# An LSTM over 512 steps: two of four gates computed with the weights stationary

## The chip, the cores and the metric

The kernel runs on one core of a Trainium2 chip. The metric is device time of one execution in microseconds, lower is better. All times below are in us unless marked ns. PE is TensorE, DVE is VectorE, ACT is ScalarE, SP is SyncE; PEld is PE's load of a stationary operand.

## The reference

`x` has shape (4, 512, 256), four sequences of 512 steps of 256 features; `h0` is `cond_1024`, (4, 256). All is f32.

```python
xW = jnp.einsum('ntd,dk->tnk', x, Wx) + b          # Wx: (256, 1024)
def step(carry, xw_t):
    prev_h, prev_c = carry
    a = xw_t + prev_h @ Wh                          # Wh: (256, 1024)
    i, f, o = sigmoid(a[:, 0:256]), sigmoid(a[:, 256:512]), sigmoid(a[:, 512:768])
    g = tanh(a[:, 768:1024])
    next_c = f * prev_c + i * g
    next_h = o * tanh(next_c)
    return (next_h, next_c), next_h
out = x + hs
```

Each step needs the one before it; the input product `x @ Wx` does not.

## The kernel before, in words

**Layout.** A 256 wide vector is cut into four quadrants of 64 units (Q = 4), each of two halves of 32 (M = 2). "By rows" a tile has partition 32q + 4t + n for quadrant q, step t of a chunk and sequence n, and 64 columns, the units of the quadrant. "By units" partition 32q + r holds unit r of quadrant q and the columns are steps and sequences. DVE's 32x32 block transpose (L296) turns the first into the second. Eight steps of four sequences fill 32 partitions, so a chunk is eight steps (STEPS), and there are 64 chunks.

**The input product.** For a whole chunk at once PE computes `x_acc` (L346) from `x_units` and `wx`, in four pieces (PIECES) behind steps 3 to 6 of the chunk before. DVE adds the bias at step 7 (`make_x_part`, L235). At the end of step 7 PE injects the result into the four PSUM banks `gates[k]` with an identity as stationary operand (`inject`, L355), once a bank's last turn is done. SP loads `x_next` and `x_here` and stores `y_rows`, each as four DMAs a chunk (L149, L154, L160).

**A step on PE** (L360 to L383). The banks are F, A, B, O; A holds G and I of half 0, B holds G and I of half 1. `recur(b, k)` takes half b of h as stationary operand (a window of `h_pad` of 32 columns in which the four of this step stand at the right place and the others are zero) and streams 64 columns of `wh`, one matmul for each of four 32-column tiles of the array.
**A step on DVE** (L280 to L327). Its order is written out: turn F, turn A, turn B (L296), `forget` (L301, it forms (tanh_f + 1) times half of c), turn O, `update(0)`, `update(1)` (a scan that gives the new cell state, L307), `hidden(0)`, `hidden(1)` (the new h into `h_pad`, L314). Step 0 begins with `turn_back` of the chunk before (L270), step 1 with `residual` (L277), step 2 with the turn of the next x (L290), step 7 with `make_x_part`. `update` waits for ACT's tanh of I and G (L305) and for `forget` (L306).

**A step on ACT** (L199 to L216). tanh_f for both halves (L203), tanh of G and I of half 0 and of half 1 (L210), tanh_o (L212), tanh of the cell for each half (L215), and half of c kept for the next step (L216). Sigmoids are tanh with halved weights. Eight instructions a step, in this order, each behind its semaphore.

Of the kernel before, what the change touches and what calls it, by code (L numbers as in the profile page):

```python
# [5 lines left out]
def lstm_residual_kernel(nc: bass.Bass, x: bass.AP, cond: bass.AP, w_x: bass.AP, w_h: bass.AP, bias: bass.AP,  # L6
                         out: bass.AP):

# [18 lines left out]
    BF, BA, BB, BO = range(4)  # L27
    BANKS = (BF, BA, BB, BO)
    GC = len(BANKS) * W
# [5 lines left out]

    PIECES = [(b, slice(c * GC // 2, (c + 1) * GC // 2)) for b in range(M) for c in range(2)]
    FIRST_PIECE_AT = 3

    ctx = ExitStack()
    with ctx:  # L40
# [12 lines left out]
        wh = sb("wh", [128, M, Q, GC])  # L53
        bias_raw = sb("bias_raw", [128, NG, QD])
# [8 lines left out]
        x_part = sb("x_part", [128, GC])  # L63

# [12 lines left out]
        gates = [ps(f"gates{k}", [128, 512]) for k in BANKS]  # L77
        x_acc = ps("x_acc", [128, 512])
        turned_bank = [ps(f"turned_bank{k}", [128, 512]) for k in range(3)]
        turned = [turned_bank[k][:, 0:W] for k in (0, 1, 2)] + [turned_bank[0][:, W:2 * W]]  # L80
        tanh_c = [turned_bank[AB[m]][:, W:W + N] for m in range(M)]
# [17 lines left out]
        x_part_made = sem("x_part_made")  # L99
        h_turned_back = sem("h_turned_back")  # L100
        y_made = sem("y_made")
        y_stored = sem("y_stored")

        gates_done = [sem(f"gates_done{k}") for k in BANKS]
        gates_turned = [sem(f"gates_turned{k}") for k in BANKS]
        tanh_f_done = sem("tanh_f_done")
        tanh_ig_done = [sem(f"tanh_ig_done{m}") for m in range(M)]
        kept_done = sem("kept_done")
        forgotten = sem("forgotten")
# [74 lines left out]
        def _(act):  # L184
# [34 lines left out]
        def _(dve):  # L219
# [8 lines left out]

            def permute_matrix(made, raw, b, factor, loaded):
# [24 lines left out]
            permute_matrix(wh, wh_raw, 0, 0.5, wh_loaded).then_inc(wh_made, 1)  # L254
            dve.wait_ge(bias_made, 1)
            make_x_part(0)
            permute_matrix(wh, wh_raw, 1, 0.5, wh_loaded).then_inc(wh_made, 1)

# [21 lines left out]
            def step(chunk, t, first, ahead):  # L280
# [10 lines left out]
                if ahead and t == STEPS - 1:  # L291
                    make_x_part(chunk + 1)

# [4 lines left out]
                def forget():  # L298

                    dve.wait_ge(tanh_f_done, now)  # L300
                    nc.vector.scalar_tensor_tensor(out=scan_both[:, :, K * N + K - 1:2 * K * N:K], in0=tanh_f[:], scalar=1.0,  # L301
                                                   in1=half_d[:], op0=ALU.add, op1=ALU.mult).then_inc(forgotten, 1)
# [36 lines left out]
        def _(pe):  # L339
# [45 lines left out]
            for piece in PIECES:  # L385
                x_product(*piece, 0)
# [33 lines left out]
```

## Time and profile before

| | |
|---|---|
| median of 3 runs | 1100.56 us (1094.28, 1100.56, 1101.48) |
| the profiled execution | 1090.95 us |
| its span, first to last instruction | 1089.2 us |
| granted TensorE clock, mean | 0.963 |
| busy: PE, PEld, DVE, ACT | 697.3, 574.9, 790.8, 550.4 us |

The time of a run is taken around the program, the span within it. The engines overlap, so busy times don't add up to the span. PE's clock is granted at one of two levels, 2.4 GHz (1.0) or 1.2 GHz (0.5).

### The profile page before, as it was taken

The page shows a single profiled execution, that of the slowest core. Times are in us where ns is not written, and L with a number is a line of the kernel's source. Part 1 is how long each engine was busy: PE and PEld are TensorE (multiplying, and loading weights), DVE is VectorE, ACT ScalarE, POOL GpSimd, SP SyncE. Part 2 cuts the span into 40 slices and gives each one's busy share as a digit, 9 for nine tenths or more (in the row PEclk, how much of TensorE's full clock was granted, in tenths as well). Part 3 has the DMA queues.
Part 4 walks back from the last instruction along what each step waited for, and adds up shares of the span by engine and source line. Part 5 has one row for each costly group of instructions (what it writes and reads, how often), then busy time and mean ns, then how long its engine had stood idle before and what let it go on. Part 6 is the DMA issues. An engine that isn't in the chain of part 4 may idle for free.

```text
span 1089.2 us, 88137 instructions
## 1 busy us (share of the span) xinstructions
PE 697.3 (64%) x36864; PEld 574.9 (53%) x36864; DVE 790.8 (73%) x4897; ACT 550.4 (51%) x3586; POOL 0.7 (0%) x6
## 2 busy tenths in 40 slices
PE   4666666666666666666666666667666666766664
PEld 3555555555555555555555555555555555545554
DVE  4777777777777777777776777776777777777776
ACT  2455555555545555555554555554545555455554
POOL 0000000000000000000000000000000000000000
PEclk9999999999999999999998999998999998999999
DMA  3000000000000000000000000000000000000000
GB/s 89 5 7 5 6 6 6 6 6 5 7 5 6 7 5 5 6 6 6 6 6 6 5 6 7 5 6 6 6 6 6 6 6 6 5 6 6 6 6 7
DMA packets 32110, 8.74 MB, mean 8 GB/s; under 512 B 31584, under 2 KB 31584, under 8 KB 32096
## 3 DMA queue, kind: packets, MB, share of 16 engines
q1 hardware_dynamic: 31488, 8.41, 3.5%
q10 hardware_dynamic: 608, 0.14, 0.1%
q8 instruction: 9, 0.15, 0.1%
q14 instruction: 5, 0.04, 0.0%
HBM read 6.43 MB, written 2.10 MB: 8 GB/s over the span
## 4 chain that ended last, share of the span: by engine, by line
DVE 51%; PE 24%; ACT 14%; issue 8%; SPq 1%; DVEq 1%; DMA 0%
DVE turned_bank L296 39%; PE gates L364 24%; DVE h_pad L314 8%; ACT tanh_o L212 8%; ACT turned_bank L215 7%; DVE scan_both L301 3%; DVE cell L307 1%; DVEq L330 1%; SPq L139 1%; DVE h_rows L270 0%; DMA wh_raw<-in_L_cond_Wh_dram 0%; SPq L143 0%; DVEq L269 0%; DVE wh L225 0%; DVE wh L222 0%
## 5 line engine op out<-in xcount | busy, mean ns | idle before, releaser
L364 PE MATMUL gates<-wh,h_pad 128*32 128x64 f32 x32768 | 591.2, 227 | 374.8 <-DVE h_pad L314 373.3
L364 PEld LDWEIGHTS gates<-wh,h_pad 128*32 128x32 f32 x32768 | 506.5, 114 | 488.3 <-DVE h_pad L314 486.4
L296 DVE STREAM_TRANSPOSE turned_bank<-gates 128x64 f32<-128x64 f32 x2048 | 478.5, 262 | 182.3 <-PE gates L364 170.0
L203 ACT ACTIVATE tanh_f<-turned_bank 128x8 f32<-128x8 f32 x512 | 90.7, 177 | 438.1 <-DVE turned_bank L296 427.6
L210 ACT ACTIVATE scan_both<-turned_bank 128x8 f32<-128x8 f32 x1024 | 185.1, 181 | 59.9 <-DVE turned_bank L296 17.3
L314 DVE SCALAR_TENSOR_TENSOR h_pad<-tanh_o,turned_bank 128x4 f32<-128x4 f32 x1024 | 132.7, 158 | 74.2 <-ACT turned_bank L215 4.6
L307 DVE TENSOR_TENSOR_SCAN cell<-scan_both 128x12 f32<-128x12 f32 x1024 | 144.0, 181 | 2.1 <-issue 0.3
L215 ACT ACTIVATE turned_bank<-cell 128x4 f32<-128x4 f32 x1024 | 143.3, 172 | 2.5 <-DVE cell L307 0.3
L346 PE MATMUL x_acc<-wx,x_units 128*32 128x128 f32 x2048 | 107.5, 285 | 9.3 <-DVE x_units L249 9.3
L212 ACT ACTIVATE tanh_o<-turned_bank 128x8 f32<-128x8 f32 x512 | 90.7, 177 | 28.9 <-DVE turned_bank L296 6.7
L216 ACT ACTIVATE half_d<-cell 128x8 f32<-128x8 f32 x512 | 100.4, 196 | 0.0
L301 DVE SCALAR_TENSOR_TENSOR scan_both<-tanh_f,half_d 128x8 f32<-128x8 f32 x512 | 77.8, 152 | 0.0
L355 PE MATMUL gates<-x_part,ident 128*32 128x64 f32 x2048 | 57.1, 230 | 1.8 <-DVE x_part L235 1.8
L346 PEld LDWEIGHTS x_acc<-wx,x_units 128*32 128x32 f32 x2048 | 50.4, 115 | 9.3 <-DVE wx L227 9.3
L355 PEld LDWEIGHTS gates<-x_part,ident 128*32 128x32 f32 x2048 | 40.6, 109 | 10.6 <-issue 2.2
L270 DVE STREAM_TRANSPOSE h_rows<-h_pad 128x64 f32<-128x64 f32 x64 | 15.7, 246 | 26.0 <-DVE h_pad L314 25.6
L235 DVE TENSOR_TENSOR x_part<-x_acc,bias_rows 128x256 f32<-128x256 f32 x64 | 26.7, 418 | 0.0
L290 DVE STREAM_TRANSPOSE x_units<-x_next 128x64 f32<-128x64 f32 x63 | 15.5, 246 | 0.0
L277 DVE SCALAR_TENSOR_TENSOR y_rows<-h_rows,x_here 128x64 f32<-128x64 f32 x64 | 14.4, 225 | 0.0
L222 DVE TENSOR_SCALAR wx<-wx_raw 128x256 f32<-128x256 f32 x2 | 0.6, 294 | 5.2 <-DMA wx_raw<-in_L_cond_Wx_dram 5.2
L193 ACT ACT_TABLE_LOAD x1 | 1.3, 1283 | 4.2 <-issue 4.2
L222 DVE TENSOR_SCALAR wh<-wh_raw 128x256 f32<-128x256 f32 x2 | 0.6, 294 | 3.0 <-DMA wh_raw<-in_L_cond_Wh_dram 3.0
(24 smaller groups left out, 6.7 us busy)
## 6 DMA issues: line engine op xcount, KB each, us to landing
x_next<-in_x_dram SPq DMA_DIRECT2D x256, 8.0 KB
x_here<-in_x_dram SPq DMA_DIRECT2D x256, 8.0 KB
out_dram<-y_rows SPq DMA_DIRECT2D x256, 8.0 KB
wx_raw<-in_L_cond_Wx_dram SPq DMA_DIRECT2D x8, 128.0 KB, 3.4
wh_raw<-in_L_cond_Wh_dram SPq DMA_DIRECT2D x8, 128.0 KB, 2.7
bias_raw<-in_L_cond_b_dram ACTq DMA_DIRECT2D x4, 32.0 KB, 3.1
h_rows<-in_cond_dram ACTq DMA_DIRECT2D x4, 1.0 KB
```

Of the source, the lines that this page charges most:

```text
L203: nc.scalar.activation(tanh_f[:], of_step(BF, t), ACT.Tanh).then_inc(tanh_f_done, 1)
L210: nc.scalar.activation(ig, of_step(AB[m], t), ACT.Tanh).then_inc(tanh_ig_done[m], 1)
L212: nc.scalar.activation(tanh_o[:], of_step(BO, t), ACT.Tanh)
L215: nc.scalar.activation(tanh_c[m], cell[:, m, :, K - 1], ACT.Tanh, scale=0.5).then_inc(tanh_done[m], 1)
L216: nc.scalar.activation(half_d[:], cell[:, :, :, K - 1], ACT.Copy, scale=0.5).then_inc(kept_done, 1)
L296: nc.vector.transpose(turned[k], gates[k][:, 0:W]).then_inc(gates_turned[k], 1)
L301: nc.vector.scalar_tensor_tensor(out=scan_both[:, :, K * N + K - 1:2 * K * N:K], in0=tanh_f[:], scalar=1.0, in1=half_d[:], op0=ALU.add, op ...
L307: nc.vector.tensor_tensor_scan(cell[:, m, :, :].rearrange("p n k -> p (n k)"), scan_in[m][:, 0:K * N], scan_in[m][:, K * N:2 * K * N], 0.0 ...
L314: nc.vector.scalar_tensor_tensor(out=h_at(m, t), in0=tanh_o[:, m, :], scalar=1.0, in1=tanh_c[m], op0=ALU.add, op1=ALU.mult).then_inc(h_don ...
L346: last = nc.tensor.matmul(x_acc[q * R:(q + 1) * R, columns], x_units[:, b * R:(b + 1) * R], wx[:, b, q, columns], start=opens, stop=b == M ...
L355: nc.tensor.matmul(gates[k][q * R:(q + 1) * R, 0:W], ident[:, q * R:(q + 1) * R], x_part[:, columns_of(k)], start=True, stop=False, tile_p ...
L364: last = nc.tensor.matmul(gates[k][q * R:(q + 1) * R, 0:W], h_stationary(b, t), wh[:, b, q, columns_of(k)], start=False, stop=b == M - 1, ...
```

## The change

F and O are computed by units: blocks of `wh` of 32 columns are the stationary operand and the four columns of h of this step are streamed. The result stands in PSUM by units in four banks of its own, one per gate and half, and needs no turn. F keeps four tiles of 32 columns; O takes two tiles of 64 columns, from a second copy of its weights, `wh_o`. A and B (I and G) stay by rows. A is turned to PSUM, B to SBUF, and so is the tanh of the cell of half 1. The x part of F and O is turned once a chunk (`turn_x_part`). F's tanh and `forget` are split by half. PE's order in a step is new, the x product has two calls instead of four pieces (behind steps 3 and 4), and `make_x_part` moves from step 7 to step 6. The two waits ahead of the scan change places. Of the pairs of load and matmul that a step has (64 before), 32 are left by rows, 32 are F by units and 16 are O by units.

Names, PSUM and buffers:

```diff
-    BF, BA, BB, BO = range(4)
+    BA, BB, BF, BO = range(4)
+    ROWS = (BA, BB)
-    PIECES = [(b, slice(c * GC // 2, (c + 1) * GC // 2)) for b in range(M) for c in range(2)]
-    FIRST_PIECE_AT = 3
+    X_PRODUCT_AT = (3, 4)
+    X_PART_AT = STEPS - 2
+    UNIT_COLUMNS = slice(GC - 4 * R, GC)
...
-        gates = [ps(f"gates{k}", [128, 512]) for k in BANKS]
+        gates = {k: ps(f"gates{k}", [128, 512]) for k in ROWS}
+        f_units = [ps(f"f_units{m}", [128, 512]) for m in range(M)]
+        o_units = [ps(f"o_units{m}", [128, 512]) for m in range(M)]
...
+        turned = {BA: a_bank[:, 0:W], BB: sb("turned_b", [128, W])[:]}
+        tanh_c = [a_bank[:, W:W + N], sb("tanh_c1", [128, N])[:]]
```

A step on ACT:

```diff
-                    act.wait_ge(gates_turned[BF], now)
-                    nc.scalar.activation(tanh_f[:], of_step(BF, t), ACT.Tanh).then_inc(tanh_f_done, 1)
                     for m in range(M):
+                        act.wait_ge(f_done[m], now)
+                        nc.scalar.activation(tanh_f[:, m, :], f_units[m][:, t * N:(t + 1) * N], ACT.Tanh).then_inc(tanh_f_done[m], 1)
                         act.wait_ge(gates_turned[AB[m]], now)
...
-                    act.wait_ge(gates_turned[BO], now)
-                    nc.scalar.activation(tanh_o[:], of_step(BO, t), ACT.Tanh)
                     for m in range(M):
+                        act.wait_ge(o_done[m], now)
+                        nc.scalar.activation(tanh_o[:, m, :], o_units[m][:, t * N:(t + 1) * N], ACT.Tanh).then_inc(o_tanh_done, 1)
                         act.wait_ge(cell_done[m], now)
```

On DVE:

```diff
+            def turn_x_part(chunk):
+                dve.wait_ge(x_part_made, chunk + 1)
+                nc.vector.transpose(x_part_units[:], x_part[:, UNIT_COLUMNS]).then_inc(x_part_turned, 1)
...
-                if ahead and t == STEPS - 1:
+                if ahead and t == X_PART_AT:
                     make_x_part(chunk + 1)
+                if ahead and t == X_PART_AT + 1:
+                    turn_x_part(chunk + 1)
...
                 def update(m):
+                    dve.wait_ge(forgotten[m], now)
                     dve.wait_ge(tanh_ig_done[m], now)
-                    dve.wait_ge(forgotten, now)
...
-                turn(BF)
                 turn(BA)
+                forget(0)
                 turn(BB)
-                forget()
-                turn(BO)
                 update(0)
+                forget(1)
                 update(1)
                 hidden(0)
                 hidden(1)
```

A step on PE:

```diff
+                def units(b, bank, k, m):
+                    at = k * W + m * R
+                    for q in range(Q):
+                        last = nc.tensor.matmul(bank[q * R:(q + 1) * R, t * N:(t + 1) * N], wh[:, b, q, at:at + R],
+                                                h_at(b, t - 1), start=False, stop=b == M - 1,
+                                                tile_position=(0, q * R), skip_group_check=True)
+                    return last
+
+                def o_part(b, m):
+
+                    for p in range(Q // 2):
+                        last = nc.tensor.matmul(o_units[m][p * 2 * R:(p + 1) * 2 * R, t * N:(t + 1) * N],
+                                                wh_o[:, b, m, p * 2 * R:(p + 1) * 2 * R],
+                                                h_at(b, t - 1), start=False, stop=b == M - 1,
+                                                tile_position=(0, p * 2 * R), skip_group_check=True)
+                    return last
+
                 pe.wait_ge(h_done[0], now)
-                recur(0, BF)
+                rows(0, BA)
+                units(0, f_units[0], BF, 0)
+                rows(0, BB)
                 pe.wait_ge(h_done[1], now)
-                recur(1, BF).then_inc(gates_done[BF], 1)
-                for k in (BA, BB, BO):
-                    recur(0, k)
-                    recur(1, k).then_inc(gates_done[k], 1)
-                if t == STEPS - 1 and ahead:
-                    pe.wait_ge(x_part_made, chunk + 2)
-                    for k in BANKS:
+                rows(1, BA).then_inc(gates_done[BA], 1)
+                units(1, f_units[0], BF, 0).then_inc(f_done[0], 1)
+                rows(1, BB).then_inc(gates_done[BB], 1)
+                units(0, f_units[1], BF, 1)
+                units(1, f_units[1], BF, 1).then_inc(f_done[1], 1)
+                if t == 0:
+                    for m in range(M):
+                        inject_o(m)
+                for m in range(M):
+                    o_part(0, m)
+                    o_part(1, m).then_inc(o_done[m], 1)
+                if ahead and t in X_PRODUCT_AT:
+                    x_product(X_PRODUCT_AT.index(t), chunk + 1)
+                if ahead and t == STEPS - 1:
+                    for k in ROWS:
                         pe.wait_ge(gates_turned[k], now)
-                        inject(k)
-                if ahead and 0 <= t - FIRST_PIECE_AT < len(PIECES):
-                    x_product(*PIECES[t - FIRST_PIECE_AT], chunk + 1)
+                    for m in range(M):
+                        pe.wait_ge(tanh_f_done[m], now)
+                    pe.wait_ge(x_part_turned, chunk + 2)
+                    inject_early()
```

`rows(b, k)` is `recur(b, k)` under a new name. `inject_early` injects A and B by rows (16 pairs) and F by units (16 pairs); `inject_o` injects one half of O with two 64-column tiles (4 pairs). Both use the identity. Ahead of the first step DVE also makes `wh_o` (two instructions) and turns the first x part.

## Rows read from the trace of the kernel before

**Rows 1.** The page: the span, and each engine's busy time and instructions

```profile
span 1089.2 us, 88137 instructions
PE 697.3 (64%) x36864; PEld 574.9 (53%) x36864; DVE 790.8 (73%) x4897; ACT 550.4 (51%) x3586; POOL 0.7 (0%) x6
```

**Rows 2.** The page: chain that ended last, shares of the span by line

```profile
DVE turned_bank L296 39%; PE gates L364 24%; DVE h_pad L314 8%; ACT tanh_o L212 8%; ACT turned_bank L215 7%; DVE scan_both L301 3%; DVE cell L307 1%; DVEq L330 1%; SPq L139 1%; DVE h_rows L270 0%; DMA wh_raw<-in_L_cond_Wh_dram 0%; SPq L143 0%; DVEq L269 0%; DVE wh L225 0%; DVE wh L222 0%
```

**Rows 3.** Order of time, one step: start, duration, engine, line, operation [idle before]

```profile
502.12 0.26 DVE L314 SCALAR_TENSOR_TENSOR h_pad<-tanh_o,turned_bank 128x4 f32<-128x4 f32 x2
...
502.33 0.94 PEld L364 LDWEIGHTS gates<-wh,h_pad 128*32 128x32 f32 x64 [1.08 <-DVE h_pad L314]
502.33 1.10 PE L364 MATMUL gates<-wh,h_pad 128*32 128x64 f32 x64 [0.92 <-DVE h_pad L314]
502.83 0.71 DVE L296 STREAM_TRANSPOSE turned_bank<-gates 128x64 f32<-128x64 f32 x3 [0.26 <-PE gates L364]
503.13 0.18 ACT L203 ACTIVATE tanh_f<-turned_bank 128x8 f32<-128x8 f32 x1 [0.81 <-DVE turned_bank L296]
503.36 0.40 ACT L210 ACTIVATE scan_both<-turned_bank 128x8 f32<-128x8 f32 x2
503.45 0.15 DVE L301 SCALAR_TENSOR_TENSOR scan_both<-tanh_f,half_d 128x8 f32<-128x8 f32 x1
503.50 0.27 DVE L296 STREAM_TRANSPOSE turned_bank<-gates 128x64 f32<-128x64 f32 x1
503.71 0.28 DVE L307 TENSOR_TENSOR_SCAN cell<-scan_both 128x12 f32<-128x12 f32 x2
503.80 0.18 ACT L212 ACTIVATE tanh_o<-turned_bank 128x8 f32<-128x8 f32 x1
503.93 0.28 ACT L215 ACTIVATE turned_bank<-cell 128x4 f32<-128x4 f32 x2
504.14 0.26 DVE L314 SCALAR_TENSOR_TENSOR h_pad<-tanh_o,turned_bank 128x4 f32<-128x4 f32 x2
```

**Rows 4.** Order of time, cut at 502.385: loads begun by then

```profile
502.33 0.16 PEld L364 LDWEIGHTS gates<-wh,h_pad 128*32 128x32 f32 x8 [1.08 <-DVE h_pad L314]
```

**Rows 5.** Order of time, step 3: a piece of the x product

```profile
505.27 0.40 PE L346 MATMUL x_acc<-wx,x_units 128*32 128x128 f32 x8
```

**Rows 6.** Order of time, eight steps apart and around a chunk's end

```profile
498.09 0.26 DVE L314 SCALAR_TENSOR_TENSOR h_pad<-tanh_o,turned_bank 128x4 f32<-128x4 f32 x2
...
512.54 0.42 DVE L235 TENSOR_TENSOR x_part<-x_acc,bias_rows 128x256 f32<-128x256 f32 x1
...
513.46 0.77 PEld L355 LDWEIGHTS gates<-x_part,ident 128*32 128x32 f32 x32
...
514.38 0.26 DVE L314 SCALAR_TENSOR_TENSOR h_pad<-tanh_o,turned_bank 128x4 f32<-128x4 f32 x2
...
515.23 0.58 DVE L296 STREAM_TRANSPOSE turned_bank<-gates 128x64 f32<-128x64 f32 x3
```

**Rows 7.** Three stretches (engines' busy time, granted clock); two turns in the second

```profile
core 0: us, PE busy (x) PEld busy (x) DVE busy (x) ACT busy (x) POOL busy (x), PEclk, DMA share, GB/s
517.41:520.82 3.41, 1.58 (x100) 1.25 (x92) 2.73 (x18) 2.15 (x14) 0.00 (x0) 1.00 0.03 7
520.83:524.24 3.41, 3.00 (x108) 2.54 (x104) 1.70 (x10) 1.01 (x7) 0.00 (x0) 0.50 0.03 7
513.99:517.40 3.41, 2.29 (x136) 1.90 (x134) 2.42 (x18) 1.57 (x12) 0.00 (x0) 1.00 0.00 0
...
521.25 0.27 DVE L296 STREAM_TRANSPOSE turned_bank<-gates 128x64 f32<-128x64 f32 x1 [0.56 <-PE gates L364]
...
521.67 0.27 DVE L296 STREAM_TRANSPOSE turned_bank<-gates 128x64 f32<-128x64 f32 x1 [0.16 <-PE gates L364]
```

**Rows 8.** Order of time: the first and the last step's hidden state

```profile
17.73 0.25 DVE L314 SCALAR_TENSOR_TENSOR h_pad<-tanh_o,turned_bank 128x4 f32<-128x4 f32 x2 [0.18 <-ACT turned_bank L215]
...
1083.94 0.26 DVE L314 SCALAR_TENSOR_TENSOR h_pad<-tanh_o,turned_bank 128x4 f32<-128x4 f32 x2
```

More of the change, by code:

```diff
@@ L63, in lstm_residual_kernel @@
         x_part = sb("x_part", [128, GC])
+        x_part_units = sb("x_part_units", [128, UNIT_COLUMNS.stop - UNIT_COLUMNS.start])
         tanh_f = sb("tanh_f", [128, M, N])
@@ L99, in lstm_residual_kernel @@
         x_part_made = sem("x_part_made")
+        x_part_turned = sem("x_part_turned")
         h_turned_back = sem("h_turned_back")
@@ L254, in _ @@
             permute_matrix(wh, wh_raw, 0, 0.5, wh_loaded).then_inc(wh_made, 1)
+            make_wh_o(0).then_inc(wh_made, 1)
             dve.wait_ge(bias_made, 1)
             make_x_part(0)
+            turn_x_part(0)
             permute_matrix(wh, wh_raw, 1, 0.5, wh_loaded).then_inc(wh_made, 1)
+            make_wh_o(1).then_inc(wh_made, 1)
             dve.wait_ge(h0_loaded, Q * DMA)
@@ L296, in turn, with forget @@
                     nc.vector.transpose(turned[k], gates[k][:, 0:W]).then_inc(gates_turned[k], 1)
[L298 to L302, printed above, removed]
+                def forget(m):
+                    dve.wait_ge(tanh_f_done[m], now)
+                    nc.vector.scalar_tensor_tensor(out=scan_in[m][:, K * N + K - 1:2 * K * N:K], in0=tanh_f[:, m, :], scalar=1.0,
+                                                   in1=half_d[:, m, :], op0=ALU.add, op1=ALU.mult).then_inc(forgotten[m], 1)
                 def update(m):
+                    dve.wait_ge(forgotten[m], now)
                     dve.wait_ge(tanh_ig_done[m], now)
-                    dve.wait_ge(forgotten, now)
                     nc.vector.tensor_tensor_scan(cell[:, m, :, :].rearrange("p n k -> p (n k)"), scan_in[m][:, 0:K * N],
@@ L339, in _, with x_product @@
         def _(pe):
-            def x_product(b, columns, chunk):
-                opens = (b, columns) == PIECES[0]
-                if opens:
+            def x_product(b, chunk):
+                if b == 0:
                     pe.wait_ge(x_turned, chunk + 1)
                 for q in range(Q):
-                    last = nc.tensor.matmul(x_acc[q * R:(q + 1) * R, columns], x_units[:, b * R:(b + 1) * R],
-                                            wx[:, b, q, columns], start=opens, stop=b == M - 1,
+                    last = nc.tensor.matmul(x_acc[q * R:(q + 1) * R, 0:GC], x_units[:, b * R:(b + 1) * R],
+                                            wx[:, b, q, :], start=b == 0, stop=b == M - 1,
                                             tile_position=(0, q * R), skip_group_check=True)
-                if (b, columns) == PIECES[-1]:
+                if b == M - 1:
                     last.then_inc(x_acc_done, 1)
@@ L357, in inject, with inject_units, inject_o @@
                                      tile_position=(0, q * R), skip_group_check=True)
+            def inject_units(bank, k, m):
+                at = k * W + m * R - UNIT_COLUMNS.start
+                for q in range(Q):
+                    nc.tensor.matmul(bank[q * R:(q + 1) * R, 0:R], ident[:, q * R:(q + 1) * R],
+                                     x_part_units[:, at:at + R], start=True, stop=False,
+                                     tile_position=(0, q * R), skip_group_check=True)
+            def inject_o(m):
+                at = BO * W + m * R - UNIT_COLUMNS.start
+                for p in range(Q // 2):
+                    nc.tensor.matmul(o_units[m][p * 2 * R:(p + 1) * 2 * R, 0:R], ident[:, p * 2 * R:(p + 1) * 2 * R],
+                                     x_part_units[:, at:at + R], start=True, stop=False,
+                                     tile_position=(0, p * 2 * R), skip_group_check=True)
@@ L359, in step, with inject_early, rows @@
+            def inject_early():
+                for k in ROWS:
+                    inject(k)
+                for m in range(M):
+                    inject_units(f_units[m], BF, m)
             def step(chunk, t, ahead):
                 now = chunk * STEPS + (t + 1)
-                def recur(b, k):
+                def rows(b, k, columns=slice(0, W)):
                     for q in range(Q):
-                        last = nc.tensor.matmul(gates[k][q * R:(q + 1) * R, 0:W], h_stationary(b, t),
-                                                wh[:, b, q, columns_of(k)], start=False, stop=b == M - 1,
+                        last = nc.tensor.matmul(gates[k][q * R:(q + 1) * R, columns], h_stationary(b, t),
+                                                wh[:, b, q, k * W + columns.start:k * W + columns.stop],
+                                                start=False, stop=b == M - 1,
```

40 lines of the change are left out of this document (25 added, 15 removed).

## The prediction

> **What bounds the kernel now.** I read the page first, then the chain, then the order of time of one step. The page shows no full engine: DVE is busy 73% of the span, PE 64%, ACT 51% [rows 1]. So it is a chain of latencies, and the chain that ended last names it: DVE's turns (L296) 39%, PE's gate matmuls 24%, then short pieces of ACT and DVE [rows 2]. The page can mislead here: DVE's turns carry the name, but the order of time shows what paces them. In one step (PE's first load at 502.33 is my zero) the three turns that follow one another take 0.71 for durations of 0.27, so they start 0.22 apart [rows 3]. At a chunk's start, where PE is ahead, three turns take 0.58, which is 0.155 apart [rows 6]. DVE could do it in 0.155; it waits for PE. PE runs 64 load-and-matmul pairs in 1.10: a round of four column tiles every (1.10 - 0.24)/15 = 0.057, I use 0.056; a gate is four rounds, 0.22 [rows 3]. The fourth turn (503.50) is also where PE's sixteenth round lets it start: 0.03 + 16 x 0.056 + 0.25 = 1.18 after zero. The 0.25 is the time from the end of a round to the turn, from the first one: 502.83 - 502.33 = 0.50 = 0.03 + 4 x 0.056 + 0.25. A step is 504.14 - 502.12 = 2.02 [rows 3]; eight take 514.38 - 498.09 = 16.29 [rows 6], 2.036 on average.
>
> Prices from the same rows: hidden's start to PE's load 0.21; turn to tanh 0.30; scan to tanh_c 0.22; tanh_c to hidden 0.21; ACT to its next instruction 0.12 (503.80 to 503.93, the pairs 0.11 apart); turn to forget 0.17, forget to the next turn 0.05; tanh of I and G to scan 0.23 (503.58 to 503.81).
>
> The rest is the clock. The steps alone give 511 x 2.036 = 1040.4; the first hidden starts at 17.7 and 5.3 follow the last [rows 8]; with the 1.75 that the profiled execution's 1090.95 has over its span that is 1065.2. The missing 26 us are stretches at 1.2 GHz: between 520.83 and 524.24 the clock is 0.50 and two turns lie 0.42 apart, twice the usual [rows 7], so a round is 0.107 there. Ahead of it, at full clock, PE was busy 1.58 of 3.41 us; after a stretch with 2.29 of 3.41 it kept the clock [rows 7].
>
> **What each step of PE costs after the change.** Rows calls (A, B) keep rounds of 0.056. The calls by units load the same 32 columns per tile but stream 4 columns, not 64. The trace has no such matmul. Below, a round can't beat its four loads: eight loads start within 0.05 (0.16 less 0.11 for one) [rows 4], so 0.028 a round. Above, it costs at most a round of 64 columns, 0.056; that it is the streamed columns that cost shows in the x products, whose second round of 128 columns comes 0.11 after the first (0.40 = 0.27 + 0.02 + 0.11) [rows 5]. I take the middle, 0.042, and keep both ends. The O tiles load 64 columns, two tiles per round: 0.055, between 0.028 and 0.11.
>
> The new step, from PE's first load. Half 0 of h: rows A 0.11, units F0 0.08, rows B 0.11, from 0.03 to 0.34 (the second h arrives at 0.28, as worked out below, so it isn't late). Rows A of half 1: 0.45, plus 0.25: turn A at 0.70. This is the change's cost: before, the first gate turned at 0.50. Units F0 end at 0.53; a short matmul and the semaphore to ACT take 0.21 (0.22 of a matmul, less its streaming, plus what a turn waits): tanh_f0 0.74, forget(0) 0.95 and, since DVE holds turn B behind it, turn B 1.00. ACT: tanh of A at 1.00 (turn A + 0.30), tanh_f1 1.12, tanh of B 1.28 (turn B + 0.28, written to SBUF), tanh_o0 1.40. PE: B done 0.64, F1 0.81, O0 0.98 plus 0.26 = 1.24, ahead of tanh_o0 by 0.16. update(0) at 1.28: tanh of A plus 0.28. Swapped waits cost or give 0.07 at most, from 0.21 as for tanh_c to 0.28; I take the dear end, since at 0.21 update(0) gains but tanh_c0 waits for tanh_o0 anyway, 0.02 in all. tanh_c0 is the later of 1.28 + 0.22 and 1.40 + 0.12: 1.52. hidden(0) 1.73, next load 1.94 to 1.95. Side path: update(1) 1.57, tanh_c1 1.79, hidden(1) 2.01, which PE sees 0.28 into the next step. What goes is two turns of DVE (F and O) and eight of PE's sixteen 64-column rounds, of which only the four ahead of the last turn were on the chain; what is late next is ACT's queue of nine instructions. With 0.028 the step is 1.92, with 0.056 1.99.
>
> Per chunk there come: the 0.16 by which eight steps exceed 8 x 2.016 [rows 6], of which 0.04 is L235 (0.42 on DVE ahead of the first turn) and now hides before the later turn A: 0.12 stay. The new turn of x_part at step 7 hides there too (0.27 for 64 columns, some 0.35 for 128, against 0.70 - 0.08). At the chunk's start the loop's end and turn_back let DVE turn first at 515.23, 0.75 after hidden(1) at 514.48 [rows 6]. hidden(1) now comes 0.28 after hidden(0): 1.03, while turn A is due at 0.21 + 0.70 = 0.91: 0.12 lost, where before it was caught up by closer turns. PE has 32 injections behind the tanh_f1 of step 7 (wait met at 1.35), five waits in a row and the loop's branch. The old ones spread over 0.77 behind four turns [rows 6]; the next step is due at 1.95. Between nothing and 0.35; with DVE's 0.12 beside it I take 0.05 more. inject_o adds four rounds ahead of O0 at step 0, 0.22 against 0.16 spare: within the DVE loss. x products: two of two rounds of 256 columns, 4 x 0.22 in all, beside tanh and scan, done by 1.7. SP's DMAs and waits don't move. Sum 0.29, I use 0.30.
>
> 8 x 1.947 + 0.30 = 15.88, or 1.985 a step; x 511 = 1014.3. Start 17.7 + 0.7 (make_wh_o twice, turn_x_part: three DVE instructions, at most 0.42 each [rows 6]); end 5.3; outside 1.75: 1039.8.
>
> The clock in this sum is full all through. PE now works from 0 to 1.2 plus a matmul's tail, about 1.4 of 1.95 with something in flight, 72% against the 46% ahead of the drop [rows 7]. So I count the 26 us as gained. If none were, 1065.
>
> The shown median is 1100.56, 0.9% over the profiled 1090.95. I put that on more time at the low clock and carry little of it over: 1042.
>
> **The skill against it.** The trace has one tile shape only, 128x32 [rows 3]; O brings 128x64 and goes back. The Trainium skill, "TensorEngine Tiling (Array Packing)", Key Properties: changing the tiling mode, not just the tile, drains the engine. No row shows it; the first rival below is its result. Also, PE pairs start 0.015 apart in four column tiles [rows 3]. The Trainium skill, "TensorE: Matmul & The Clock Gate", Part 1, has a floor of about 25 ns between starts however few the columns. The trace disagrees already; by it a units round would be 0.10, the step 2.25 and the time 1196 (an estimate from that page); I give it 0.03.
>
> **Rivals.** (1) Slower: O is late. Before O's first load PE waits until what flies has ended, at most a matmul's 0.22, plus the load, and the same again before the next 32-column tiles. Place: ACT's queue, where tanh_o0 stands ahead of tanh_c0. Forecast O0 1.24, needed 1.40; every 0.01 beyond goes into the step, and from O0 = 1.50 (with 2.05 a step) nothing is left of the gain even with the clock. With 0.30 of wait and 0.042: 1.54, step 2.09, chunk 17.0, time 1111; with 0.056: 1161; with 0.028: 1061. For it: a new shape; against: PE is idle anyway before the next step. (2) Slower too: the clock falls to 1.2 GHz over long stretches, since PE streams half the columns of before and its matmuls of 4 columns load it little. Rounds are then 0.107, those by units some 0.056, and the same chain gives a step of about 2.5: 1329 throughout, 1185 if half the time. For it: the clock of before already drops after the emptier stretches [rows 7]; against: PE's busy share rises. (3) The change doesn't do what it says: rounds of 4 columns cost as much as those of 64. PE then runs 24 rounds of 0.056 ahead of O, where all four gates took 16: step 1.99, 1061; and without the clock's gain 1087, no change.
>
> **Chances.** Forecast 0.55 (1014 to 1065); rival 1 0.20; rival 2 0.10; rival 3 0.12; the 25 ns floor 0.03. A measurement tells about 1% here. Faster by over 1%: the forecast, half of rival 1, nearly all of rival 3: 0.75. Within 1%: 0.08. Slower: the other part of rival 1, rival 2, the floor: 0.17. Range 1010 to 1130: below, 0.028 and only 0.13 per chunk give 1016; above, rival 1's middle.
>
> **What would show it.** Turn A 0.70 after PE's first load, turn B 0.30 later; tanh_o0 right behind tanh of B, not idle for PE; step 1.95; clock above 0.99. Wrong if the PE matmuls to f_units start over 0.05 a round apart, if O's first load waits 0.2, or if the low clock takes over 10% of the span.

## The result, and the profile after

The changed kernel takes 1460.84 us (four runs, 1460.77 to 1460.90) against 1097.42 of the kernel before (1087.36 to 1101.48): 1.333 times, interval 1.323 to 1.343. The forecast was 1042, faster, with 1010 to 1130. It went the other way. Below, a time is the median of all runs of a kernel, while a ratio leaves out runs over 1.5% above that kernel's fastest.

The page after: span, busy time of the engines, and the chain by line.

```profile
span 1459.0 us, 104138 instructions
...
PE 1405.5 (96%) x44544; PEld 1306.1 (90%) x44544; DVE 761.5 (52%) x4451; ACT 690.1 (47%) x4610; POOL 0.7 (0%) x6
...
PE gates L406 37%; PE o_units L423 24%; PE f_units L415 12%; PE x_acc L369 9%; ACT tanh_o L224 4%; DVE h_pad L340 4%; PE gates L377 3%; PE o_units L391 3%; ACT a_bank L226 2%; PE f_units L384 1%; SPq L150 0%; DMA wh_raw<-in_L_cond_Wh_dram 0%; SPq L154 0%; DVE wh L236 0%; DVE wh L233 0%
```

PE is busy 96% of the span where it was 64% [rows 1], and the chain that was DVE's turns [rows 2] is PE in four lines, 37 + 24 + 12 + 9%. PE streams less: of the 64 pairs of a step with 64 columns 32 are left, and 48 pairs of 4 columns stand in place of the others. But each instruction takes longer. The same matmul of 64 columns (durations min/median/max in ns) in the kernel before, first in the step of [rows 3], then in the stretch at clock 0.50 of [rows 7]:

```profile
L364 PE MATMUL gates<-wh,h_pad x64: 219/219/243, 502.3 to 503.2; 128*32 128x64 f32 x64
...
L364 PE MATMUL gates<-wh,h_pad x48: 270/311/311, 520.8 to 522.0; 128*32 128x64 f32 x48
```

and after, in a plain step in the middle, then in the whole run:

```profile
L406 PE MATMUL gates<-wh,h_pad x32: 294/314/317, 516.0 to 517.0; 128*32 128x64 f32 x32
...
L406 PE MATMUL gates<-wh,h_pad x16384: 294/314/317, 15.5 to 1452.1; 128*32 128x64 f32 x200
```

311 to 314 ns is the duration at 1.2 GHz (clock 0.50 in the kernel before), and none of the 16384 is shorter than 294. The profile of the changed kernel holds no record of a granted clock, and its clock then reads 1.0; by the durations TensorE ran at 1.2 GHz from start to end. A plain step there, in order of time:

```profile
516.00 0.20 PEld L406 LDWEIGHTS gates<-wh,h_pad 128*32 128x32 f32 x8 [0.20 <-DVE h_pad L340]
...
516.24 0.17 DVE L340 SCALAR_TENSOR_TENSOR h_pad<-tanh_o,tanh_c 128x4 f32<-128x4 f32 x1 [0.29 <-ACT tanh_c L226]
...
517.05 0.27 DVE L322 STREAM_TRANSPOSE a_bank<-gates 128x64 f32<-128x64 f32 x1 [0.46 <-PE gates L406]
517.07 0.39 PE L415 MATMUL f_units<-h_pad,wh 128*32 128x4 f32 x16
...
517.40 0.94 PEld L423 LDWEIGHTS o_units<-h_pad,wh_o 128*64 128x64 f32 x16
517.40 1.02 PE L423 MATMUL o_units<-h_pad,wh_o 128*64 128x4 f32 x16
517.43 0.24 DVE L322 STREAM_TRANSPOSE turned_b<-gates 128x64 f32<-128x64 f32 x1
...
518.02 0.18 DVE L333 TENSOR_TENSOR_SCAN cell<-scan_both 128x12 f32<-128x12 f32 x1
...
518.32 0.16 DVE L340 SCALAR_TENSOR_TENSOR h_pad<-tanh_o,a_bank 128x4 f32<-128x4 f32 x1
518.47 0.17 ACT L224 ACTIVATE tanh_o<-o_units 128x4 f32<-128x4 f32 x1 [0.18 <-PE o_units L423]
518.53 0.20 PEld L406 LDWEIGHTS gates<-wh,h_pad 128*32 128x32 f32 x8 [0.20 <-DVE h_pad L340]
```

The step, from one first load to the next, is 2.53 (518.53 - 516.00). O's 16 pairs take 0.94 to load, a round of two 64-column loads every 0.107, and tanh_o of half 1 waits for them (518.47, released by `o_units`). Steps 3 and 4 are worse:

```profile
700.84 0.16 DVE L340 SCALAR_TENSOR_TENSOR h_pad<-tanh_o,a_bank 128x4 f32<-128x4 f32 x1
700.88 0.20 PEld L369 LDWEIGHTS x_acc<-wx,x_units 128*32 128x32 f32 x8
700.88 1.08 PE L369 MATMUL x_acc<-wx,x_units 128*32 128x256 f32 x8
...
701.31 0.20 PEld L406 LDWEIGHTS gates<-wh,h_pad 128*32 128x32 f32 x4 [0.23 <-issue]
...
701.73 0.20 PEld L406 LDWEIGHTS gates<-wh,h_pad 128*32 128x32 f32 x4 [0.23 <-issue]
```

The x product streams two rounds of 256 columns, 0.427 each at this clock, and the next step's second set of loads waits for it from 701.31 to 701.73: 3.20 instead of 2.53. From hidden(0) to hidden(0) a chunk has five steps of 2.53, two of 3.20 and one of 3.48, 22.5 in all, 2.81 a step; 511 of them and the start and end give the 1459 of the span. The kernel before, had it never left 1.2 GHz, would take 2.79 a step (three steps that lay wholly in such stretches took 2.791 to 2.794), 1450 us. That is an estimate from three plain steps; its steps with the x product and the injections were never seen there and are likely longer. So at the low clock the two are about alike, and the plain step of the changed one is the shorter.

### The profile page after: what moved, and what is told of

It reads as the page before. It is cut to its first block, busy times and chain, and to the rows that moved or that the text cites. A ratio compares the mean times of both kernels' runs of the same rounds, so it can differ in the third digit from the quotient of the medians.

```text
span 1459.0 us, 104138 instructions
## 1 busy us (share of the span) xinstructions
PE 1405.5 (96%) x44544; PEld 1306.1 (90%) x44544; DVE 761.5 (52%) x4451; ACT 690.1 (47%) x4610; POOL 0.7 (0%) x6
## 4 chain that ended last, share of the span: by engine, by line
PE 87%; ACT 6%; DVE 4%; issue 2%; SPq 1%; DMA 0%; DVEq 0%
PE gates L406 37%; PE o_units L423 24%; PE f_units L415 12%; PE x_acc L369 9%; ACT tanh_o L224 4%; DVE h_pad L340 4%; PE gates L377 3%; PE o_units L391 3%; ACT a_bank L226 2%; PE f_units L384 1%; SPq L150 0%; DMA wh_raw<-in_L_cond_Wh_dram 0%; SPq L154 0%; DVE wh L236 0%; DVE wh L233 0%
## 5 line engine op out<-in xcount | busy, mean ns | idle before, releaser
L423 PE MATMUL o_units<-h_pad,wh_o 128*64 128x4 f32 x8192 | 522.6, 250 | 0.0
L415 PEld LDWEIGHTS f_units<-h_pad,wh 128*32 128x32 f32 x16384 | 522.0, 172 | 0.0
L415 PE MATMUL f_units<-h_pad,wh 128*32 128x4 f32 x16384 | 497.2, 202 | 0.0
L423 PEld LDWEIGHTS o_units<-h_pad,wh_o 128*64 128x64 f32 x8192 | 482.1, 223 | 7.7
L215 ACT ACTIVATE tanh_f<-f_units 128x4 f32<-128x4 f32 x1024 | 177.2, 173 | 556.3 <-PE f_units L415 551.4
L322 DVE STREAM_TRANSPOSE a_bank<-gates 128x64 f32<-128x64 f32 x512 | 135.9, 265 | 348.5 <-PE gates L406 348.5
L224 ACT ACTIVATE tanh_o<-o_units 128x4 f32<-128x4 f32 x1024 | 177.2, 173 | 185.9 <-PE o_units L423 129.7
L327 DVE SCALAR_TENSOR_TENSOR scan_both<-tanh_f,half_d 128x4 f32<-128x4 f32 x1024 | 169.4, 165 | 16.5
L369 PE MATMUL x_acc<-wx,x_units 128*32 128x256 f32 x1024 | 138.4, 635 | 9.3 <-DVE x_units L270 9.3
L322 DVE STREAM_TRANSPOSE turned_b<-gates 128x64 f32<-128x64 f32 x512 | 124.5, 243 | 0.0
```

The source lines that it names most:

```text
L215: nc.scalar.activation(tanh_f[:, m, :], f_units[m][:, t * N:(t + 1) * N], ACT.Tanh).then_inc(tanh_f_done[m], 1)
L224: nc.scalar.activation(tanh_o[:, m, :], o_units[m][:, t * N:(t + 1) * N], ACT.Tanh).then_inc(o_tanh_done, 1)
L322: nc.vector.transpose(turned[k], gates[k][:, 0:W]).then_inc(gates_turned[k], 1)
L327: nc.vector.scalar_tensor_tensor(out=scan_in[m][:, K * N + K - 1:2 * K * N:K], in0=tanh_f[:, m, :], scalar=1.0, in1=half_d[:, m, :], op0=A ...
L369: last = nc.tensor.matmul(x_acc[q * R:(q + 1) * R, 0:GC], x_units[:, b * R:(b + 1) * R], wx[:, b, q, :], start=b == 0, stop=b == M - 1, ti ...
L415: last = nc.tensor.matmul(bank[q * R:(q + 1) * R, t * N:(t + 1) * N], wh[:, b, q, at:at + R], h_at(b, t - 1), start=False, stop=b == M - 1 ...
```

## The experiments

**1. Bring the clock up with matmuls that compute nothing.** A filler is 8 pairs of load and matmul into an unused part of the bank gates A. As it stands in `g1_hold` (group 4); the runs differ in the number of columns and in the steps that have it:

```diff
+            def filler(start=False, n=192):
+                for _ in range(1):
+                    for q in range(Q):
+                        nc.tensor.matmul(gates[BA][q * R:(q + 1) * R, GC:GC + n], ident[:, q * R:(q + 1) * R],
+                                         wx[:, 0, q, 0:n], start=start, stop=start,
+                                         tile_position=(0, q * R), skip_group_check=True)
...
                     o_part(1, m).then_inc(o_done[m], 1)
+                if t < STEPS - 1:
+                    pe.wait_ge(gates_turned[BA], now)
+                    filler(n=128 if t in X_PRODUCT_AT else 192)
```

In `e1_fill128` and `e2_fill256` it ran in every step, with `start=True`. That spoils the sums in gates A, so the values these two compute are not those of the LSTM. The full-clock plain step is 2.03 in them and in `g1_hold`, which has `start=False`, so the times may be used.

> The changed kernel, with 8 more pairs of load and matmul a step (identity as stationary operand, 128 columns streamed into an unused part of the bank gates A) after O. They compute nothing that is used. Theory CLOCK (the whole loss is that TensorE ran at 1.2 GHz from start to end): the clock comes up, a round of 64 columns takes 0.056 instead of 0.107, the step is 1.95 to 2.0 and the time 1040 to 1080. Theory SHAPE (the loss is O's loads of 64 columns and the change of tile shape, whatever the clock): the fillers change no load of O; the time stays above 1400. If the clock doesn't come up with 128 columns, the fillers only add work: 1480 to 1560.

Measured: 1123.25 (1112.9 to 1134.1), 1.022 (1.016 to 1.027) of before, clock 0.948.

> As the run with 128 columns, with 256 columns per filler. Theory CLOCK: the clock comes up; the fillers take 0.43 a step at 2.4 GHz and end near 1.95, so they may push the next step by up to 0.1: 1045 to 1110. Theory SHAPE: above 1500. If this run comes up and the one with 128 does not, the clock is decided by how much the fillers stream.

Measured: 1138.21, 1.043 (1.036 to 1.050), clock 0.992. Eight pairs more a step take 320 to 340 us away. Theory SHAPE is out; the clock was the loss. But 1123 is not 1040 to 1080, nor 1138 within 1045 to 1110. At full clock the plain step is 2.03, not 1.95, and the filler of step 7 costs 0.2 to 0.5 at each chunk's start (2.33 and 2.54 there). With 256 columns the two steps right after the x products take 2.24 as well. And the profiled run of `e1_fill128` spent some 143 us at 1.2 GHz, where eight steps take 25.0 instead of 16.5: about 49 us of its 1127 (an estimate from these step times).

> The changed kernel with 96 more pairs of 256 columns (some 10 us at 1.2 GHz, less at 2.4) once, ahead of the first step, none in the steps. If the clock only had to be brought up once: 1050 to 1070. If the steps themselves can't hold it: it is at 2.4 GHz for the first few steps and falls, and the time is 1465 to 1475, the burst's own length over the changed kernel.

Measured: 1464.79, one run. The burst brings the clock up, and it falls after 10 us. Engines' busy time and granted clock of two stretches of this run:

```profile
core 0: us, PE busy (x) PEld busy (x) DVE busy (x) ACT busy (x) POOL busy (x), PEclk, DMA share, GB/s
18.00:28.00 10.00, 8.70 (x350) 7.01 (x346) 3.74 (x25) 3.57 (x27) 0.00 (x0) 1.00 0.02 5
28.20:38.20 10.00, 9.89 (x288) 8.80 (x280) 4.96 (x30) 4.57 (x31) 0.00 (x0) 0.50 0.03 7
```

**2. O in 32-column tiles.** In `e4_o32` O uses `units(b, o_units[m], BO, m)`, and `inject_units` instead of `inject_o`.

> The changed kernel with O in four tiles of 32 columns like F (32 pairs of load and matmul a step instead of 16; inject_o by 32-column tiles too), no fillers: no change of tile shape is left. The clock stays at 1.2 GHz. Theory CLOCK: 4-column rounds of four 32-column loads take 0.054 at 1.2 GHz and O's rounds of two 64-column loads 0.107, so O ends 0.5 earlier and tanh_o waits for ACT instead of for PE: step 2.53 to about 2.40, time about 1390. Theory SHAPE (shape change and 64-column loads are most of the loss): below 1200.

Measured: 1430.79 (1406.7 to 1487.4), mean clock 0.694 in the profiled run. At the low clock its plain step is 2.31 to 2.35 against 2.53 (forecast 2.40), at full clock 2.03, as with 64-column tiles. So the O tiles cost 0.2 a step at 1.2 GHz and nothing at 2.4 GHz; SHAPE, which asked for under 1200, is out again. Only the steps say this, not the time, in which two things that were not expected work against each other. The clock came up for 515 us, without any filler. And 18 of the 63 later chunks began with a step of 9.0 to 10.3 instead of 2.07 (full clock) or 3.63 (low): 105 to 133 us in all. In one of them PE issues nothing for 5.16 and then 1.53 with nothing seen to wait for; the last line is the DMA queue of kind "instruction" over the whole run:

```profile
79.95 0.21 PEld L406 LDWEIGHTS gates<-wh,h_pad 128*32 128x32 f32 x8 [5.16 <-issue]
...
82.77 0.32 PE L406 MATMUL gates<-wh,h_pad 128*32 128x64 f32 x2 [1.53 <-issue]
...
q8 instruction: 175, 2.87, 1.0%
```

It moved 2.87 MB in 175 packets, against 0.18 MB in 11 in the changed kernel, and packets of it lie in these gaps. So PE most likely waited for its own program, which is 16 pairs a step longer; no run tests it. The time near the 1390 of the forecast is luck.

**3. Fillers only in plain steps, and the kernel before with fillers.** `e5_fill_plain` is the base; `e6_fill_swapback` has the two waits ahead of the scan back in their old order, `e7_fill_order` DVE's order turn(BA), turn(BB), forget(0), update(0).

> The changed kernel with fillers of 192 columns in steps 0, 1, 2, 5 and 6 only (not where the x product or the injections follow). It is the base for the next two. From the run with 128 columns in every step: a plain step is 2.03 at full clock and the chunk's start costs 0.3 more; 8 x 2.03 + 0.3 = 16.54, 2.067 a step, so 1080 to 1090 if the clock holds at 2.4 GHz. If it falls at steps without a filler: above 1110.

> The base run with the two waits ahead of the scan in the order of before. At full clock the loop that sets the step runs through half 1: hidden(1), the second h on PE, gates A, turn A, turn B behind forget(0), tanh of B, update(1), tanh_c1, hidden(1). The scan now starts 0.10 after the end of tanh of B, behind a separate wait of 0.065. If the second wait of a pair is issued as an instruction of its own, with the old order forget(1) waits there instead and the scan starts 0.03 to 0.04 earlier: step 2.00, time 14 to 20 us below the base. If the swap is free either way: equal to the base within 4 us.

> The base run with DVE's order turn A, turn B, forget(0), update(0) instead of turn A, forget(0), turn B, update(0). In the base turn B starts 0.2 after its gate is done, since forget(0) waits ahead of it for tanh_f0. Theory HALF 1 (the step is set by the loop through half 1): turn B comes 0.17 to 0.2 earlier, tanh of B goes from 1.43 to 1.27 after PE's first load, update(1) by 0.1 earlier: step 1.93 to 1.97, time 1030 to 1055. Theory HALF 0 (the loop through update(0) and hidden(0) sets it): equal to the base or up to 10 us slower.

Measured: 1608.56, 1608.51, 1608.58. The clock never rose, so the question put to the last two was not asked. What they do show: at 1.2 GHz PE sets the loop (99% of the chain that ended last, plain step 2.99), and neither edit moves the time by 0.1 us. The last of the group is the kernel before with a filler of 64 columns into `gates[BF]`:

```diff
+                if t < 3:
+                    pe.wait_ge(gates_turned[BF], now)
+                    filler()
                 if t == STEPS - 1 and ahead:
                     pe.wait_ge(x_part_made, chunk + 2)
```

> The kernel before with 8 pairs of 64 columns more in steps 0, 1 and 2 of a chunk, behind the last gate, into an unused part of the bank gates F. If its stretches at 1.2 GHz are what lies between 1091 and the 1065 that its steps sum to, the clock share is 1.0 and the time 1062 to 1070. If they have another cause: 1088 to 1100, with the drops still there.

Measured: 1067.38 (1065.7 to 1068.2), 0.977 (0.969 to 0.984):

```profile
core 0: 1063.9 us, clock 0.998
```

The sum of the prediction, 1065 without low stretches, was right, and the kernel before was itself 2.3% short of its own steps.

**4. Hold the clock, then vary one thing.** A burst of 12 fillers of 256 columns ahead of the first step, 192 columns in steps 0, 1, 2, 5, 6 and 128 in 3 and 4.

> The changed kernel with the one burst of 96 pairs of 256 columns ahead of the first step, and fillers of 192 columns in steps 0, 1, 2, 5, 6 and 128 columns in steps 3 and 4. The plain fillers alone never brought the clock up (1608 us), the burst alone brought it up for 10 us; together they should reach 2.4 GHz and hold it: plain steps 2.03, x steps 2.03, 0.3 more at a chunk's start, 2.067 a step, time 1080 to 1095, no more than 1% from before. If it falls it stays down for long stretches: above 1150.

> The held clock, with DVE's order turn A, turn B, forget(0), update(0). Theory HALF 1 (at full clock the step is set by the loop through hidden(1), gates A, turn A, turn B, tanh of B, update(1), tanh_c1): turn B 0.17 to 0.2 earlier, update(1) 0.1 earlier, step 1.93 to 1.97, 30 to 50 us below the held base. Theory HALF 0 (the loop through update(0)): equal to the base or up to 10 us slower.

> The held clock, with the two waits ahead of the scan as before. If the second wait of a pair is an instruction of its own (0.065 to the scan), forget(1) waits there instead of tanh of B and the scan starts 0.03 to 0.04 earlier: 14 to 20 us below the held base. If the swap is free either way: within 4 us of it.

> The held clock, with DVE's new order and the waits as before. With turn B early, tanh of B ends before forget(1) does, so the old order of waits puts the separate wait behind the later of the two: 0.02 to 0.07 a step slower than the new order alone, 10 to 35 us above it, if the loop runs through update(1). If both gains add up instead, 14 to 20 us below it.

Measured: g1 1089.09, 0.993 (0.986 to 1.001) of before. The other three scatter widely with the clock: g2 1064 to 1664, g3 1071 to 1665 (one run of each almost wholly at the low clock), g4 1074 to 1156. So their times are no answer. Their steps are: in each profile, the hidden-to-hidden time of full-clock steps that end in step 3, median, is 2.032 for g1, 1.921 for g2, 1.974 for g3, 1.993 for g4. In this step the order gives 0.11; the waits swapped back give 0.06 alone (forecast 0.03 to 0.04) and cost 0.07 with the new order. Not every step gains as much: the two right after the x products (2.03 and 2.04 in g2) gain nothing, and the chunk's first loses (2.09 in g1, 2.15 in g2, 2.21 in g3). The medians of all eight steps add up to 16.27, 15.91, 16.17 and 16.20. So the order is worth 0.045 a step on average, 23 us in all and not the 30 to 50 of the forecast; the waits swapped back are worth 0.012 alone, 6 us and not 14 to 20, and cost 0.036 with the new order, 18 us, as forecast. One step of g1, in order of time:

```profile
566.22 0.14 DVE L340 SCALAR_TENSOR_TENSOR h_pad<-tanh_o,a_bank 128x4 f32<-128x4 f32 x1
...
566.41 0.16 PEld L413 LDWEIGHTS gates<-wh,h_pad 128*32 128x32 f32 x8 [0.40 <-DVE h_pad L340]
...
566.58 0.16 DVE L340 SCALAR_TENSOR_TENSOR h_pad<-tanh_o,tanh_c 128x4 f32<-128x4 f32 x1 [0.21 <-ACT tanh_c L226]
...
566.96 0.16 PEld L413 LDWEIGHTS gates<-wh,h_pad 128*32 128x32 f32 x8
...
567.05 0.25 PEld L422 LDWEIGHTS f_units<-h_pad,wh 128*32 128x32 f32 x16
...
567.18 0.27 DVE L322 STREAM_TRANSPOSE a_bank<-gates 128x64 f32<-128x64 f32 x1 [0.25 <-PE gates L413]
567.27 0.17 ACT L215 ACTIVATE tanh_f<-f_units 128x4 f32<-128x4 f32 x1 [0.63 <-PE f_units L422]
567.32 0.55 PEld L430 LDWEIGHTS o_units<-h_pad,wh_o 128*64 128x64 f32 x16
...
567.48 0.16 DVE L327 SCALAR_TENSOR_TENSOR scan_both<-tanh_f,half_d 128x4 f32<-128x4 f32 x1
...
567.56 0.24 DVE L322 STREAM_TRANSPOSE turned_b<-gates 128x64 f32<-128x64 f32 x1
...
567.84 0.21 ACT L221 ACTIVATE scan_both<-turned_b 128x8 f32<-128x8 f32 x1
...
567.95 0.16 ACT L224 ACTIVATE tanh_o<-o_units 128x4 f32<-128x4 f32 x1
...
568.15 0.18 DVE L333 TENSOR_TENSOR_SCAN cell<-scan_both 128x12 f32<-128x12 f32 x1
568.25 0.14 DVE L340 SCALAR_TENSOR_TENSOR h_pad<-tanh_o,a_bank 128x4 f32<-128x4 f32 x1
568.37 0.21 ACT L226 ACTIVATE tanh_c<-cell 128x4 f32<-128x4 f32 x1
```

hidden(1) starts at 566.58; PE's second half of gates A follows, turn A 567.18, turn B 567.56, tanh of B 567.84, update(1) 568.15, tanh_c1 568.37. That is the loop that sets 2.03, half 1's; hidden(0) stands behind update(1) in DVE's order (568.15, 568.25), so half 0 can't run ahead of it. Turn B is late: forget(0) stands ahead of it at 567.48. In g2 turn B comes first:

```profile
555.69 0.16 DVE L340 SCALAR_TENSOR_TENSOR h_pad<-tanh_o,a_bank 128x4 f32<-128x4 f32 x1
...
555.90 0.16 PEld L413 LDWEIGHTS gates<-wh,h_pad 128*32 128x32 f32 x8 [0.36 <-DVE h_pad L340]
...
556.65 0.27 DVE L322 STREAM_TRANSPOSE a_bank<-gates 128x64 f32<-128x64 f32 x1 [0.30 <-PE gates L413]
...
556.84 0.25 DVE L322 STREAM_TRANSPOSE turned_b<-gates 128x64 f32<-128x64 f32 x1
...
557.01 0.12 DVE L327 SCALAR_TENSOR_TENSOR scan_both<-tanh_f,half_d 128x4 f32<-128x4 f32 x1
...
557.12 0.21 ACT L221 ACTIVATE scan_both<-turned_b 128x8 f32<-128x8 f32 x1
...
557.51 0.18 DVE L333 TENSOR_TENSOR_SCAN cell<-scan_both 128x12 f32<-128x12 f32 x1
...
557.65 0.16 DVE L340 SCALAR_TENSOR_TENSOR h_pad<-tanh_o,a_bank 128x4 f32<-128x4 f32 x1
```

Turn B is 0.19 behind turn A instead of 0.38, and the second scan starts 0.86 after turn A instead of 0.97.

**5. A denser filler, and which part costs the clock.** `k1_keep` has 224 columns in the plain steps and 192 behind the injections of step 7; `k2_keep_order` adds the new order. `k3_o_rows` has no filler; O is computed with `rows(0, BO)`, `rows(1, BO)` and turned on DVE ahead of update(1). `k4_o_rows_order` adds the new order.

> The changed kernel with a denser filler: the burst, 224 columns in steps 0, 1, 2, 5 and 6, 128 in steps 3 and 4, and 192 behind the injections of step 7, where PE is idle during the loop's branch; the last chunk is filled too. The drops of the held runs began around a chunk's start, so they should go. Then every run lies close to the sum of full-clock steps: 6 x 2.03 + 2 x 2.03 + 0.1, 2.04 to 2.05 a step, 1075 to 1085 us, clock above 0.99. If the drops stay: runs spread over more than 20 us.

> The same with DVE's order turn A, turn B, forget(0). Full-clock steps of the held run with this order were 1.92 (steps 1, 3, 7), 1.97 to 2.04 (2, 4, 5, 6) and 2.15 (0): 15.9 a chunk, 1.99 a step, 1045 to 1055 us, 30 below the run without it and 0.955 to 0.965 of the kernel before. If fillers of 224 columns come into the way of the shorter step: 1060 to 1075.

Measured: k1 1094.28, 1.002 (0.999 to 1.005), of 14 runs; k2 1071.57, 0.979 (0.974 to 0.984), clock 0.997 in the profiled run. The drops did not all go: k1 spreads from 1090 to 1137, with five runs above 1105, and two of the six runs of k2 lie at 1095 and 1101. Plain steps are as forecast. The time is some 14 over the middle of it in k1 and some 20 in k2, where it lies in the second range (1060 to 1075), since the filler behind the injections is on the way after all: 2.35 and 2.37 at each chunk's start against 2.09 and 2.15. The order gives 23 us between the two, as the steps of g1 and g2 say.

> The changed kernel with O by rows again (64 columns streamed, its turn on DVE before update(1), one tanh_o), F by units, no fillers. Theory COLUMNS (the clock fell because PE streams half the columns): with three gates of four by rows again the clock comes up and holds for part or most of the time: 1085 to 1200. Theory UNITS (short matmuls of 4 columns as such, of F too, keep the clock down): it stays at 1.2 GHz, above 1400.

> As the run with O by rows, with DVE's order turn A, turn B, forget(0). Where the clock is up the step is 1.92 to 1.97 instead of 2.03, as in the held runs; the time is 20 to 50 us below the run with O by rows if both hold the clock alike. The turn of O may push update(1) by up to 0.1, since turn B, forget and turn O now all lie ahead of it: then equal.

Measured: 1273.69 and 1275.29, 1.163 and 1.164.

```profile
core 0: 1273.9 us, clock 0.835
```

With O's 64 columns streamed again and F still by units, the clock is up two thirds of the time; theory UNITS is out. COLUMNS is not shown by that: the time lies outside its 1085 to 1200 too, and the clock of `e4_o32`, which streams 4 columns for O, was up for 37% of its span. Where the clock of k3 and k4 is up the step is 2.20, for both orders. In both, ACT waits for turn O, which stands behind forget(1) on DVE, and tanh_c0 and hidden(0) follow. From k3:

```profile
753.81 0.26 DVE L322 STREAM_TRANSPOSE o_bank<-gates 128x64 f32<-128x64 f32 x1
...
754.10 0.18 ACT L223 ACTIVATE tanh_o<-o_bank 128x8 f32<-128x8 f32 x1 [0.20 <-DVE o_bank L322]
```

With the new order ACT waits 0.32 there, so turn B's gain is lost again.

**6. The best of it.** The burst earlier, 256 columns in steps 0 and 6, nothing (`m1_best`) or 96 columns (`m2_best96`) behind the injections, new order.

> The new DVE order (turn A, turn B, forget(0)) with the burst moved ahead of the wait for the first x part (10 fillers of 256 columns instead of 12), fillers of 256 columns in steps 0 and 6, 224 in 1, 2 and 5, 128 in 3 and 4, none behind the injections. In the kept run those behind the injections cost 0.2 at each chunk's start (2.37 against 2.15), 13 us in all. Without them, and with a start 4 us shorter: 1047 to 1057 where the clock holds all through; it may fall at some chunk's start, then 1070 to 1110 in such runs.

> The same with 96 columns behind the injections: the chunk's start costs about half of the 0.2 again, 1053 to 1063, and the clock holds in more of the runs. Both should be faster than the kernel before (1092) and than its filled version (1067).

Measured: m1 1080.34 with runs from 1054.6 to 1708.9; m2 1101.65 with runs from 1068.8 to 1725.6. The low end of m1 is what was forecast (1047 to 1057), and no run of another kernel was below it; but one run of m1 and two of m2 stay at 1.2 GHz, and where they fall was not settled. So neither is shown to be faster than 1067. The versions that beat both kernels in measurement are `e8_before_fill`, 1066 to 1068 in its four runs, and `k2_keep_order`, 1072 with two of six runs at 1095 and more.

## Why the prediction was wrong

**The clock, the step that failed.** "The clock in this sum is full all through", and "72% against the 46% ahead of the drop [rows 7]. So I count the 26 us as gained." The clock was never full. At full clock all through the changed kernel would take some 1065 (an estimate: 16.27 for eight steps from g1, the changed kernel's own start and end), so of the 419 us between 1042 and 1461 the clock is about 396 and the mis-sized step 23. The share of time in which PE has something in flight does not tell it. A fall in g1:

```profile
39.10:42.50 3.40, 2.44 (x120) 2.02 (x112) 1.85 (x12) 1.59 (x12) 0.00 (x0) 1.00 0.00 0
42.50:45.90 3.40, 3.34 (x96) 3.14 (x100) 1.56 (x10) 1.35 (x9) 0.00 (x0) 0.50 0.02 5
```

It followed 3.40 us of which PE was busy 2.44, more than the 2.29 of [rows 7] after which the kernel before kept its clock. The changed kernel had PE busy 96% and never got it. The Trainium skill, "TensorE: Matmul & The Clock Gate", Part 1, ties the clock to how busy PE has been and warns of idle gaps; PE had hardly one here, and the clock was low. The measurement decides. The busy row is not the activity: the record of a 4-column matmul is 0.17 long at full clock, almost as long as the 0.22 of one with 64 columns. What does bring the clock up is open. It rose with a filler in every step, and for part of the time with O by rows; but it also came up for 37% of the span of `e4_o32`, which has neither and streams hardly more than the changed kernel, and it never rose in `e5_fill_plain`, which has fillers in five steps of eight. Rival 2's reason, fewer columns, is thus not shown; its low clock is. Rival 2 named the low clock, at 0.10 and with 1329 us throughout. Its plain step, "about 2.5", was 2.53; it lacked the x products and injections, which at this clock come onto the chain: 0.67 twice and 0.95 once a chunk, 2.3 x 64 = 147 us.

**The step at full clock, mis-sized.** Forecast 1.95, measured 2.03, which takes the gain in the steps away: eight full-clock steps of g1 take 16.27, against 16.29 in the kernel before [rows 6]. Even with the clock held the change by itself would gain nothing, and with the new order of DVE 0.36 in a chunk. By terms, from PE's first load at 566.41 in g1:
- Units rounds: 0.042 taken, 0.028 found; 16 loads of F1 take 0.25. But the load of the first such round behind streamed ones starts after a full 0.056. The lower bound was right, and rival 3 is out. (It has "24 rounds of 0.056 ahead of O"; there are 16, and 24 with O's eight.)
- Turn A: 0.70 forecast, 0.77 measured. Not PE's rounds but the second h: "the second h arrives at 0.28" was 0.38 (hidden(1) 566.58 and 0.21 on). The loop runs through half 1, which I called the side path.
- Turn B: 1.00 forecast, 1.15 measured, from the later turn A, tanh_f0 and forget(0).
- update(1): 1.57 forecast, 1.74 measured. Tanh of B reads SBUF and takes 0.21, not 0.18, tanh_c1 writes SBUF and takes 0.21, not 0.17. The swap of the waits, counted at 0.02 "in all", lies on this path: 0.06 in the steps that end in step 3, 0.012 on average.
- O: rounds of two 64-column loads 0.055 forecast, (0.55 - 0.14) / 7 = 0.059 measured. (The forecast's "O0 0.98" is 0.81 and four rounds of 0.042, not of its own 0.055; with that it is 1.03, and still not late.) tanh_o0 1.54 against 1.40, right behind tanh of B as said.

**Rival 1, the change of tile shape.** At full clock O's first load starts at 567.32, 0.13 after F's last (which ends at 567.30, 0.11 long). Without a change the next round of units would start some 0.03 after it, so about 0.10 more. The Trainium skill, "TensorEngine Tiling (Array Packing)", Key Properties, has the engine drain there; the trace agrees that something waits. It cost nothing in the full-clock step: with O in 32-column tiles that was the same 2.03.

**The 25 ns floor**, which the prediction takes from the Trainium skill, "TensorE: Matmul & The Clock Gate", Part 1, was rightly given little: pairs start 0.007 apart, taking the four column tiles in turn. But one and the same tile gets a pair only every 0.028 in the units rounds. Counted by tile the trace does not contradict the floor; the prediction counted it over four tiles.

**Per chunk and start.** 0.30 was forecast; in g1 eight steps take 16.27, which is 0.03 over 8 x 2.03. The start went as said: the first hidden at 18.2 (forecast 18.4), 5.6 behind the last (5.3).

## What to carry to other kernels

When a change makes PE's matmuls shorter, ask for the clock first: price the new kernel at 1.2 GHz too, and give that case weight if the old one already drops at times. A higher share of busy time is no argument that the clock will hold. A PE row busy 96% with matmul durations of the low clock is the sign, even where the profile prints a clock of 1.0. With two interleaved halves, work the loop out for each; the one with the longer way round sets the step, and DVE's written order can make a finished gate wait. Judge such an edit by all steps of a chunk, not by the one that gains most: 0.11 in one was 0.045 on average.

## What was not expected

- A profile without any clock record reads as clock 1.0; e5 printed 1.0 at 1608 us, k3 printed 0.835 at 1274.
- Matmuls that compute nothing made the kernel before 2.3% faster, 1067 against 1095.
- With the same code the clock can stay low for nearly a whole run: g2 ran in 1064 and in 1664 us. It need not: in the profile of g1 it fell at 42.5 and was back after 41 us.
- `e4_o32` lost over 100 us at chunk starts, with sixteen times the bytes in the instruction queue.
